# A fused two-layer kernel of gated attention and routed experts on one core: the first batch's router later in the order, a weight ring of seven places instead of four, and the row scatter in two halves

## What is computed

```python
x = x + tanh(g_xattn[0]) * L0_xattn(ctx, ctx, masks, norm(x))    # scores times norm(x), masked, softmax
x = x + tanh(g_ffn[0])   * L0_ffn(norm(x))     # shared expert + router + 8 experts, all computed, top 2 weighted
x = x + tanh(g_xattn[1]) * L1_xattn(norm(x), ctx)     # 16 heads with latent keys and rotary positions
x = x + tanh(g_ffn[1])   * L1_ffn(norm(x))     # router, top 2 of 8 experts of 256, silu gate, clipped at 7
```

## Time and profile before

| | us |
|---|---|
| median of 3 runs (lowest, highest) | 488.09 (485.65, 489.6) |
| the profiled execution, whole | 487.2 |
| its span | 485.4 |
| PE busy / DVE busy / ACT busy / POOL busy | 406.5 (84%) / 326.4 (67%) / 234.5 (48%) / 135.7 (28%) |
| mean granted clock of PE in the span | 0.933 of 2.4 GHz |

### The profile page before, as it was taken

The page is one execution under the profiler, slowest core; times in us unless marked ns, Lnnn a source line. Parts: engine busy times, 40 slices in busy tenths (PEclk is TensorE's granted clock), DMA queues, the critical chain, the costliest instruction groups (busy, mean ns, idle before and its releaser), DMA issues.

```text
span 485.4 us, 7933 instructions
## 1 busy us (share of the span) xinstructions
PE 406.5 (84%) x2691; PEld 334.2 (69%) x2691; DVE 326.4 (67%) x772; ACT 234.5 (48%) x515; POOL 135.7 (28%) x140
## 2 busy tenths in 40 slices
PE   1669896668799988998998898779898689999996
PEld 0334485336579777888777797669897468778885
DVE  0889259653799666999459995668662347555885
ACT  1022179233559647298455695552463165444322
POOL 5716000002601126302056011235177460000640
PEclk9999569796759999999999999998999799999999
DMA  6994700018001001001000010042242532211330
GB/s 159 292 341 144 99 1 1 0 52 273 22 2 45 1 1 44 2 23 23 2 22 24 1 45 1 2 109 76 78 132 105 177 113 85 88 65 46 92 106 22
DMA packets 30744, 35.37 MB, mean 73 GB/s; under 512 B 5713, under 2 KB 25793, under 8 KB 30449
## 3 DMA queue, kind: packets, MB, share of 16 engines
q1 hardware_dynamic: 26304, 28.11, 19.4%
q0 software_dynamic: 4400, 6.75, 6.3%
HBM read 25.61 MB, written 7.60 MB: 68 GB/s over the span
## 4 chain that ended last, share of the span: by engine, by line
PE 48%; DVE 26%; ACT 7%; issue 5%; DMA 2%; POOL 2%; SPq 0%; DVEq 0%; ACTq 0%; POOLq 0%
DVE egh L1727 11%; PE bank L1501 8%; PE bank L1363 6%; PE bank L1525 6%; DVE negm L1808 5%; PE bank L1178 4%; ACT Qs L972 3%; PE bank L1303 3%; PE bank L1322 2%; PE bank L1342 2%; PE bank L1343 2%; PE bank L1149 2%; PE bank L1127 2%; POOL xs L751 2%; PE bank L1164 1%
## 5 line engine op out<-in xcount | busy, mean ns | idle before, releaser
L1727 DVE RECIPROCAL egh<-egh 128x256 bf16<-128x256 bf16 x44 | 76.6, 1742 | 15.4 <-ACT egh L907 15.4
L1363 PE MATMUL bank<-kv,probs 128*128 128x128 f32 x512 | 67.5, 275 | 3.7 <-ACT negmT L964 2.9
L1363 PEld LDWEIGHTS bank<-kv,probs 128*128 128x128 f32 x512 | 62.5, 192 | 4.4 <-issue 3.5
L991 ACT ACTIVATE probs<-bank 128x512 f32<-128x512 f32 x64 | 36.9, 587 | 17.5 <-PE bank L1343 17.5
L1808 DVE TENSOR_REDUCE negm<-bank 128x2 f32<-128x512 f32 x64 | 41.4, 686 | 4.0 <-PE bank L1322 3.8
L1322 PE MATMUL bank<-Kh,Qs 128*128 128x256 f32 x128 | 32.7, 350 | 9.7 <-DVE negm L1808 4.8
L731 POOL TENSOR_SCALAR veps<-mv 128x2 f32<-128x2 f32 x12 | 2.7, 225 | 133.6 <-DVE mv L1559 133.6
L1342 PE MATMUL bank<-Qs,Kh 128*128 128x256 f32 x128 | 39.4, 329 | 0.0
L742 POOL TENSOR_TENSOR W<-w_in,W 128x512 fp32r<-128x512 f32 x24 | 30.0, 1282 | 32.9 <-issue 24.8
L1525 PEld LDWEIGHTS bank<-W,hTs 128*128 128x128 f32 x210 | 28.1, 189 | 15.5 <-DVE hTs L1962 9.9
L1525 PE MATMUL bank<-W,hTs 128*128 128x256 f32 (+1 forms) x210 | 32.9, 292 | 6.0 <-DVE hTs L1962 4.8
(11 more groups left out here) (205 smaller groups left out, 889.9 us busy)
## 6 DMA issues: line engine op xcount, KB each, us to landing
Qm<-Qs SPq DMA_DIRECT2D x32, 128.0 KB
xs<-f3A SPq DMA_DIRECT2D x1, 2432.0 KB, 9.7
Qm<-xs SPq DMA_DIRECT2D x19, 128.0 KB, 2.3
ys<-y SPq DMA_DIRECT2D x19, 128.0 KB, 2.0
w_q<-in_wq SPq DMA_DIRECT2D x2, 1024.0 KB, 17.9
w_o<-in_woT SPq DMA_DIRECT2D x1, 2048.0 KB, 10.9
w_in<-in_L_ffn_Wg SPq DMA_DIRECT2D x8, 256.0 KB, 4.2
w_in<-in_L_ffn_Wu SPq DMA_DIRECT2D x8, 256.0 KB, 2.7
```

The lines of the kernel that those rows point to most:

```text
L991: done(act.activation(flat(pT[:, n % 3]), bank1(b, FILL_ST + h)[:], ACT.Exp), "p_ready")
L1363: ins = pe.matmul(bank_v(b, h // 2)[:, at:at + P], pT[:, n % 3, lt, t * P:(t + 1) * P], kv_all[:, frm:frm + P], start=(lt == 0), stop=(lt ...
L1727: done(dve.reciprocal(eg[:, j], eg[:, j]), "e1")
```

## The change

Three parts. (1) In `run_all` and in `ffn0` on four engines: for the first batch the router, the turning of `hs` and its copies come behind the fourth of the eleven blocks (`LATE = 3`) instead of ahead of the first, and blocks stand between the quarters of `fold`; three of the four steps that make `Go` come behind the keys and ahead of the last block's reciprocal. (2) `NWIN` is 7: SP issues seven loads at once early on, all up to load 21 ahead of the fetches of rows, and 22 and 23 behind four of them; ACT's high parts of experts 6 and 7 come ahead of the first tile's tanh. (3) `scatter` takes a range: six DMAs ahead of the split of expert 4, six behind it. The head of batch 2 is taken one step of the attention earlier.

```diff
--- before.py
+++ after.py
@@ -79,12 +79,16 @@
     take(f)
     take(scores)
     take(f)
+    take(fo)
+    take(f, 2)
+    take(fo)
+    take(f, 2)
+    take(fo)
+    take(fo)
+    spread(f, J0 - 3, fo, 5)
+    take(ks, None)
     take(fo, 3)
-    take(f)
-    take(fo)
-    spread(f, J0 + 1, fo, 5)
-    take(ks, None)
-    spread(f, NE + 2, fo, 4)
+    spread(f, NE + 2, fo, 1)
     take(fo, None)
     for b in range(B - 1):
@@ -138,19 +142,18 @@
     take(heads[2])
     take(a, 3)
     take(heads[2])
+    take(a)
+    take(heads[2], None)
     take(a, 2)
-    take(heads[2], None)
-    take(a)
     take(p, None)
     for _ in range(3):
         take(w)
         take(a, 4)
     take(a, None)
-    take(t, 3)
     take(w)
     take(t)
     take(w)
-    take(t, 2)
+    take(t, 5)
     take(heads[3])
     take(t)
     take(heads[3])
@@ -281,7 +284,7 @@
         Bs = [folding(f"Bs{n}", [P, 512]) for n in range(2)]
         fold_space.close()
-        NWIN = 4
+        NWIN = 7
         w_in = sb("w_in", [P, NWIN, IC * H])
         NXIN = 4
@@ -424,6 +427,8 @@
         FILLS0 = J0 + NE
+
+        LATE = 3
         def wait_fill0(pe, b, i):
@@ -665,8 +670,6 @@
                 for n in range(2, 4):
                     queries_in(b, n)
                     maxima_in(b, n)
-            for k in range(NWIN, 7):
-                load_w1(k)
             for n in range(2):
                 queries_in(B - 1, n)
             for k in range(7, 10):
@@ -678,15 +681,14 @@
             for n in range(2, 4):
                 queries_in(B - 1, n)
                 maxima_in(B - 1, n)
-            for k in range(13, 18):
+            for k in range(13, 22):
                 load_w1(k)
             for i in range(NXIN):
                 load_x(i)
-            for k in range(18, 3 * NE):
+            for k in range(22, 3 * NE):
                 load_w1(k)
-                if k == 21:
-                    for i in range(NXIN, 6):
-                        load_x(i)
+            for i in range(NXIN, 6):
+                load_x(i)
             for s in range(SORTED + 3):
                 if s >= 3:
                     store_y(s - 3)
@@ -742,11 +744,11 @@
                     done(pool.tensor_tensor(w1_matrix(e, m, 1), w_in[:, k % NWIN].rearrange("p (c i) -> p c i", c=IC),
                                             w1_matrix(e, m, 0).bitcast(F32), ALU.subtract), "w1_lo")
-            def scatter():
+            def scatter(ns):
                 pool.wait_ge(S_["slots_ready"], 1)
                 pool.wait_ge(zeroed, 16)
-                for n in range(NS * T):
+                for n in ns:
                     for k in range(2):
                         pool.indirect_dma_start(xs, bass.IndirectOffsetOnAxis(slot[:, n, k:k + 1], 0),
                                                 f3_of(n // T)[:, n % T], None).then_inc(scattered, 16)
@@ -831,9 +833,10 @@
                     for e in range(3):
                         w1_split(e)
                 if n == len(LN_ORDER) - 1:
-                    for e in range(3, 5):
-                        w1_split(e)
-                    scatter()
+                    w1_split(3)
+                    scatter(range(NS))
+                    w1_split(4)
+                    scatter(range(NS, NS * T))
                     for e in range(5, NE):
                         w1_split(e)
                 rstd_of(b)
@@ -880,18 +883,28 @@
                         act.wait_ge(S_["hs_ready"], 2 * b)
                     done(act.activation(th[:, t], bank[(3, 0)[t]][:, 0:I0], ACT.Tanh, scale=0.5), "th_ready")
                 yield
-                act.wait_ge(S_["router_sb"], b + 1)
-                done(act.activation(el[:], lgm[:], ACT.Exp), "router_exp")
-                yield
-
-                act.wait_ge(S_["hsT_ready"], b + 1)
-                if b >= 1:
-                    act.wait_ge(S_["w_used"], 8 * b)
-                else:
-                    act.wait_ge(S_["mask_sum"], B)
-                done(act.activation(hsT[:, 0], bank[0][:, 0:S], ACT.Copy, scale=0.5), "hsT_sb")
-                done(act.activation(hsT[0:I0 - P, 1], bank[0][0:I0 - P, S:2 * S], ACT.Copy, scale=0.5), "hsT_sb")
-                yield
+
+                def exp_router():
+
+                    act.wait_ge(S_["router_sb"], b + 1)
+                    done(act.activation(el[:], lgm[:], ACT.Exp), "router_exp")
+
+                def copy_hs():
+
+                    act.wait_ge(S_["hsT_ready"], b + 1)
+                    if b >= 1:
+                        act.wait_ge(S_["w_used"], 8 * b)
+                    else:
+                        act.wait_ge(S_["mask_sum"], B)
+                    done(act.activation(hsT[:, 0], bank[0][:, 0:S], ACT.Copy, scale=0.5), "hsT_sb")
+                    done(act.activation(hsT[0:I0 - P, 1], bank[0][0:I0 - P, S:2 * S], ACT.Copy, scale=0.5), "hsT_sb")
+
+                if b:
+                    exp_router()
+                yield
+                if b:
+                    copy_hs()
+                    yield
                 if b == 0:
                     act.wait_ge(S_["s0_ready"], B)
                     act.wait_ge(S_["mask_f"], 2)
@@ -906,6 +919,10 @@
                     own(act, "eg_exp")
                     done(act.activation(eg[:, j], eg[:, j], ACT.Copy, bias=1.0), "eg_ready")
                     yield
+                    if b == 0 and j == LATE:
+                        exp_router()
+                        copy_hs()
+                        yield
                 yield
                 for n in range(8):
                     m = 8 * b + n
@@ -1071,7 +1088,6 @@
         PARTS = ((0, 0), (0, 1), (1, 0))
-
         @block.tensor
         def _(pe):
             def transpose_f(bk, rows_f, ready):
@@ -1128,14 +1144,20 @@
                     done(ins, "su_ready")
                 yield
                 yield
-                pe.wait_ge(S_["hs_ready"], 2 * (b + 1))
-                pe.wait_ge(S_["router_sb"], b + 1)
-                for t in range(T):
-                    pe.transpose(bank[0][:, t * P:(t + 1) * P], hs[:, t, 0:P], ident[:])
-                for t in range(T):
-                    ins = pe.transpose(bank[0][0:I0 - P, S + t * P:S + (t + 1) * P], hs[:, t, P:I0], ident[:])
-                done(ins, "hsT_ready")
-                yield
+
+                def turn_hs():
+
+                    pe.wait_ge(S_["hs_ready"], 2 * (b + 1))
+                    pe.wait_ge(S_["router_sb"], b + 1)
+                    for t in range(T):
+                        pe.transpose(bank[0][:, t * P:(t + 1) * P], hs[:, t, 0:P], ident[:])
+                    for t in range(T):
+                        ins = pe.transpose(bank[0][0:I0 - P, S + t * P:S + (t + 1) * P], hs[:, t, P:I0], ident[:])
+                    done(ins, "hsT_ready")
+
+                if b:
+                    turn_hs()
+                    yield
                 pe.wait_ge(S_["fTb_ready"], b + 1)
                 loaded(pe, "wg0", "wu0")
                 for j in range(J0):
@@ -1714,8 +1739,9 @@
                         dve.wait_ge(S_["hsT_ready"], b)
                     done(dve.scalar_tensor_tensor(hs[:, t], th[:, t], 1.0, bank[(3, 0)[t]][:, I0:2 * I0], ALU.add, ALU.mult), "hs_ready")
                 yield
-                router([bank[(3, 0)[t]][:, 2 * I0:SG] for t in range(T)], b)
-                yield
+                if b:
+                    router([bank[(3, 0)[t]][:, 2 * I0:SG] for t in range(T)], b)
+                    yield
                 yield
                 def weigh_up(j):
                     done(dve.tensor_tensor(he[:, j], eg[:, j], gu[:, j, 1, :], ALU.mult), "he_ready")
```

## The result

The changed kernel takes 473.96 us (median of four, 473.58 to 475.7), the kernel before beside it 486.87 us (485.6 to 489.6). The ratio is 0.9733 with a 95% interval of 0.97 to 0.9765: faster by 12.9 us, where 5.2 were forecast. Of the distance between 482.9 forecast and 473.96 measured, 1.2 us is the kernel before itself, which has 486.87 here and had 488.09 in the forecast; the other 7.7 are the miss.

The account below looks back on a forecast made before the run. No single engine bounds the whole (TensorE busy 84%, VectorE 67%); each stage has its own limit. Gains 2.5 + 0.4 + 2.2 + 0.1 = 5.2 us take the median from 488.1 to 482.9 us, eight in ten between 475 and 488.

Parts of the forecast that it names:

- the part on the clock: First batch's fold: TensorE's clock falls to 1.2 GHz, so the third and fourth quarters take 4.9 us each.
- rival 1: First batch's fold: clock stays at 2.4 GHz, quarters take 3.2 us; 8.0 us more gained, 474.9 us; chance 0.27.
- The path to the fifth reciprocal: First expert stage: TensorE's work sets the fifth reciprocal's start, at 73.4 us against 74.41 before.
- into time that VectorE has to spare, so cost 0: First batch: router's 2.9 us on VectorE falls between fourth and fifth reciprocal, cost 0; without that cover 2.9.
- Behind the fifth reciprocal: First expert stage: eleventh reciprocal 12.6 + 4.8 us later, down products 1.9 after it, then 12.7 to the end.
- The scatter's term: Row scatter: halves around the fifth split and an earlier third-batch choice gain 2.5 us, lower bound 1.7.
- The ring's term: Sorted tiles: seven weight places remove the stall at 397.98, gain 2.2 us, bounds 0 and 3.
- Rival 2: Sorted tiles: the weight wait only moves, to load 23 before the first tanh; 485.1 us; chance 0.13.
- The clock term: First sorted tiles' gate products: 0.4 us of clock loss won back, between 0 and 2.0.
- Rival 3: Fifth block to 92 us: clock stays low until the down products, 8 us lost, 491 us; chance 0.05.
- 2.4 GHz up to 48 us: First batch's front before the change: granted clock is 1.00 up to 48 us, then 0.50 from 52 to 56.

## Why the prediction was wrong

**The step that failed** is in the part on the clock: "I take it that it will fall again, since the new order puts only four blocks [...] among three narrow quarters." It did not fall there. With wide blocks in place of the wait of 1.78 us, the clock stayed at 2.4 GHz through both quarters and fell only behind the next wait, the 1.67 us at 56.6. The filled wait alone, in the old order, gave 7.9 us. This is rival 1, which had a chance of 0.27 and a time of 474.9 us against the measured 473.96 (a time that lies just outside the range that was said to take it in).
**The path to the fifth reciprocal** was worked out as 73.4, and as 64.8 in rival 1. It was 66.74. Quarters took 2.9, where the sums had 4.9 and 3.2; but neither sum had the new wait of 1.67 us for the router, since I priced the router only on VectorE ("into time that VectorE has to spare, so cost 0") and not as something that the turn of `hs` waits for. By the experiments it is worth some 3 us, wait and clock together (471.06 against 473.96).

**Behind the fifth reciprocal the steps held.** The eleventh came 16.3 us later (forecast 12.6 + 4.8 = 17.4 at the low clock, 16.5 at the high one), the down products 2.3 after it (1.9), the stage's rest took 12.6 (12.7). That the eleventh stands behind the low parts was right; the run that moved it, and the fifth with it, gained 3 us.

**The scatter's term** of 2.5 was 2.6 in the trace. But the forecast called it a gain of its own, and it is not: without the ring it is a loss of 3.9 us. The forecast named the fifth split as what the scatter passes, and did not ask who waits for the places that this split frees. That is the rule for a step that is moved past another: the waiters of the other must be counted too. In the changed kernel the ring hides it, so the sum was right, but by luck: nothing in the working says that one part needs the other.

**The ring's term** of 2.2 was 2.35 alone. Rival 2, a first tanh that waits for the weights, didn't happen, with 0.31 us to spare. The clock term of 0.4 was nothing at the first gate products, which take 2.93 us before and 2.91 after. At the second it is there: 2.01 us before, 1.64 after. In the table it falls into the last stretch, which gained 2.6 where 2.2 were forecast.

**Rival 3** asked for a clock of 0.50 at 76 us, and it was 0.50 from 76 to 78. But its mechanism, a clock that is still low from the front, did not come: the clock had been at 1.00 from 68 to 75 and fell again, behind a wait of TensorE of 1.86 us (the share is 0.92 over 72 to 76 and 0.65 over 76 to 80). VectorE was busy all that time, and none of the 8 us of this rival shows. As a sign to tell the rivals apart, a clock at one moment was a poor choice.

## What to carry to other kernels

Before an order is priced, look at each wait of TensorE in a stretch that TensorE bounds, and price the stretch behind it at both clocks: here filling a wait of 1.78 us gained 7.9. A cheap trial, needless products in the wait, tells in one run whether the clock is the matter, and an order that has real work there, or no wait, gives as much without them (8.9 us for the new front, 2.9 us for the router's place). Such a trial changes two things at once, the length of the wait and the work ahead of it. When two traces are compared by the microsecond, compare them from a mark that lies ahead of the edit: in these traces the front alone differs by up to 1.1 us between executions. When a step moves past another one on its queue, list who waits for the one passed: parts of a change that each look like a gain can be a loss alone and a gain only together.

## What the runs showed of the hardware

- Fall and return of the clock follow different things here. Two quarters of narrow float32 products, 5.7 us without a wide one, ran at 1.00 (from 49.95 in the kernel with the filled wait). The same products in the kernel before ran at the low clock for 9.8 us, 50.14 to 59.98, without bringing it back.
- The length of a wait did not decide by itself. Behind 14 wide products, waits of 0.63 and 1.31 us ahead of the third quarter were followed by 1.00 through two narrow quarters; 0.78 us between narrow quarters was followed by slow products within 2 us. Wide work ahead of the wait is what differs in these three rows; that it is the cause was not tried by itself.
- A front of the same instruction order ends at different times, for the most part by the clock: 97.99 and 96.26 for the changed kernel and the one that differs from it only in a head step 250 us later. TensorE's products show where 1.0 of these 1.7 us comes from (the first two lines are the changed kernel, the third is the other one):

```profile
33.00 0.69 PE L1240 MATMUL bank<-w_kqa,w_qra 128*64 128x128 f32 x2
...
39.94 5.01 PE L1143 MATMUL bank<-w_sgu,fT 128*128 128x360 f32 x8
...
39.84 4.01 PE L1143 MATMUL bank<-w_sgu,fT 128*128 128x360 f32 x8
```

  The same eight products take 5.01 us in one and 4.01 in the other. Ahead of them a pair of the fold takes 0.69 us, behind them 0.43, so by these durations the clock rises under them, at a moment that differs. The profile's granted clock is 1.00 for the whole of this time, from 0 to 48 us in both. So that row is not to be trusted ahead of its first fall; the durations of equal products are. The forecast's "2.4 GHz up to 48 us" holds by them only from about 45 us on, which its sum does not touch.
